# Mixture-of-experts products: tokens as the stationary operand in four column strips, weights as the moving one

## The chip, the cores and the metric

The kernel runs on one core of a Trainium2 chip, in one launch. The metric is the device time in microseconds (us) from the start to the end of an execution; before the change it is 238.63 us, the median of three runs (238.31 to 239.33). In the core, TensorE (PE) multiplies: a load puts a stationary operand into its 128x128 array, then a matmul streams a moving operand past it and writes into PSUM, a memory of eight banks of 512 fp32 columns on 128 partitions. VectorE (DVE) and ScalarE (ACT) read PSUM and write SBUF, the working memory; GpSimd (POOL) works on SBUF alone; DMA queues bring weights from HBM.

## The reference

A small network of two layers over 256 tokens with 192 channels. Each layer is an attention block and then a mixture of eight experts with two experts per token; this change is in the experts alone.

```python
# layer 0: hidden width h = 432, 528, 624, 752, 896, 1088, 1312, 1584
gate = softmax(x @ router.T); val, idx = top_k(gate, 2)
for e in range(8):
    w = sum(where(idx == e, val, 0))
    out += w[:, None] * ((silu(x @ gates[e].T) * (x @ ups[e].T)) @ downs[e].T)
# layer 1: hidden width 768, gates divided by the sum of the two picked
for e in range(8):
    out += tok_w[:, e:e+1] * (relu(x @ w1[e].T + b1[e]) @ w2[e].T + b2[e])
```

All products are fp32.

## The kernel before

Everything is written out by hand: each engine has its own program, in a fixed order, and waits on semaphores. Per layer: norm, attention, norm, router, then the experts. In the experts the router's picks give every token a place among up to 96 (`SLOTS`) places of its expert. PE gathers the tokens of each expert by a product with a matrix of zeros and ones (`gather`, L1183) into PSUM, four experts at a time; ACT and DVE copy the result to `xe_hi` (channels 0 to 127) and `xe_lo` (channels 128 to 191, in two halves of the partitions with zeros between, so that one product can serve gate and up at once). An expert with more than 96 tokens gets the rest in an extra pass; in this run layer 1 has one such job, at the end.

Then come steps, one for each tile of 128 hidden columns of an expert, 60 in layer 0 and 24 in layer 1 (where a step takes two tiles). In `first_products` (L1196, L1198, L1200) the weights, 128 columns of them, are the stationary operand and the 96 tokens the moving one: 96 columns for gate, 192 for the lower channels of both, 96 for up. The hidden values come out with the hidden index on partitions. ACT takes the silu (L521) and DVE the product with up (L786), or each of them adds the bias and takes the relu (L527, L789). That is already the stationary operand of `down` (L1211), with 192 columns of the down weights as the moving one. Two steps (layer 0) or one (layer 1) lie between a step's first products and its `down`, in a ring of four hidden buffers. At the end of an expert DVE copies the 96x192 sum (`y_out`, L775) and `combine` (L1219) multiplies it by the turned gates (`weightedT`: POOL writes `weighted`, L479, PE turns it, L1228, ACT or DVE copies it) into bank 4, where all experts are added up. In layer 1 `L1265` puts the second bias there first.

Every fp32 matmul of the program stands as two in the trace (a transpose as one).

Around it: the weights of all experts of layer 0 are loaded while the attention of layer 0 runs, those of layer 1 after layer 0 is done (`moe_done`), during the attention of layer 1. ACT and DVE read a register and branch before the last expert (to know whether an extra pass follows), PE branches after the last.

Of the kernel before, what the change touches and what calls it, by code (L numbers as in the profile page):

```python
# [42 lines left out]
E = 8  # L43
# [9 lines left out]

HALF = C // 2
# [18 lines left out]
def metaformer_kernel(nc, x_in, weights_hi, weights_lo, weights_mid, params, rel_in, const_in, experts0, experts1,  # L73
                      bias1_in, bias2_in, out):
    with ExitStack() as ctx:
# [66 lines left out]
        weighted = carve(TT * E * SLOTS).rearrange("p (t e s) -> p t e s", t=TT, e=E)  # L142
        weightedT = carve(E * TOK).rearrange("p (e t) -> p e t", e=E)
        xe_hi = carve(E * SLOTS).rearrange("p (e s) -> p e s", e=E)
        hidden = carve(RING * 2 * SLOTS).rearrange("p (r u s) -> p r u s", r=RING, u=2)
        silu_g = carve(2 * SLOTS).rearrange("p (r s) -> p r s", r=2)
        y_out = carve(2 * C).rearrange("p (r c) -> p r c", r=2)

        xe_lo = carve(E * 2 * SLOTS).rearrange("p (e u s) -> p e u s", e=E, u=2)

# [11 lines left out]
        carve_w0(JOB_ROOMS, SIZE1)  # L164
        job_weighted = carve_w0(JOBS, TT, SLOTS)
# [45 lines left out]
        ones_set, zeros_set, half_set = sem("ones_set"), sem("zeros_set"), sem("half_set")  # L211
# [23 lines left out]
        weightedT_psum, weightedT_act, weightedT_vec = sem("weightedT_psum"), sem("weightedT_act"), sem("weightedT_vec")  # L235
# [7 lines left out]
        main = [stream_sems(f"main{layer}") for layer in range(2)]  # L243
# [4 lines left out]

        zeros_job, jobs_ready, job_picked, job_gathered, job_x = (
# [9 lines left out]
        steps1 = [(e, t, P) for e in range(E + JOBS) for t in range(STEPS1)]  # L259
# [3 lines left out]
        main_steps = [range(first_step[layer][E]) for layer in range(2)]  # L263
        TAIL = first_step[0][E - 1]
# [25 lines left out]
        PAIR_AT = (((0, 0), (0, 3), (1, 2), (2, 0)), ((0, 0), (0, 2), (1, 1), (2, 0)))  # L290

        OVER_CHOSEN = 1 + 2 * TT
        OVER_X = 4

        def weightedT_bank(pair):
            return bank[(7, 6, 7, 7)[pair]]
# [4 lines left out]
        PICK_JOB_AT, GATHER_JOB_AT, COPY_JOB_AT = (4, 1), (5, 2), (6, 0)  # L301
# [50 lines left out]
        def tokens_of(e):  # L352

            return (xe_hi[:, e], xe_lo[:, e]) if e < E else (job_xe_hi[:, e - E], job_xe_lo[:, e - E])

        def bias1_of(e, u, t):

            at = u * STEPS1 + t
            return bias1[:, e * TILES1 + at:e * TILES1 + at + 1] if e < E else job_bias[:, e - E, at:at + 1]
# [26 lines left out]
        def _(sp):  # L386
# [8 lines left out]
            for e in range(E):  # L395
                sp.dma_start(w0[:, OFF0[e]:OFF0[e + 1]], experts0[:, OFF0[e]:OFF0[e + 1]]).then_inc(e0_landed[e], 16)
# [6 lines left out]
            for e in range(E):  # L403
                sp.dma_start(w0[:, e * SIZE1:(e + 1) * SIZE1], experts1[:, e]).then_inc(e1_landed[e], 16)

            def load_job(k):

                expert = sp.value_load(job_regs[0:1, 1 + k:2 + k], min_val=0, max_val=E - 1)
                if k >= JOB_ROOMS:

                    sp.wait_ge(main[1]["hidden_used"], first_step[1][E + k - JOB_ROOMS + 1])
# [9 lines left out]
        def _(pool):  # L421
# [6 lines left out]
            for n in range(4):  # L428
# [24 lines left out]
                else:  # L453
                    pool.wait_ge(o_psum, HG * (layer + 1))
                    pool.wait_ge(rstd_ready, n + 1)
                    for half in range(2):
                        if layer + half > 0:
                            pool.wait_ge(zeros_set, 2 * layer + half)
                        nc.gpsimd.memset(xe_lo[CL * half:CL * (half + 1), :, 1 - half, :], 0.0).then_inc(zeros_set, 1)
                    pool.wait_ge(zeros_set, 2 * layer + 2)  # L460
# [16 lines left out]
                    for e in range(E):  # L477
                        for t in range(TT):
                            nc.gpsimd.tensor_scalar(weighted[:, t, e, :], places, place[:, t, e:e + 1], gate[:, t, e:e + 1],  # L479
                                                    ALU.is_equal, ALU.mult).then_inc(weighted_ready, 1)  # L480

        @block.scalar
        def _(act):
# [24 lines left out]
            def copy_weightedT(layer, pair):  # L508
                act.wait_ge(weightedT_psum, 4 * layer + pair + 1)
                nc.scalar.copy(weightedT[0:SLOTS, 2 * pair:2 * pair + 2].rearrange("p e t -> p (e t)"),  # L510
                               weightedT_bank(pair)[0:SLOTS, :]).then_inc(weightedT_act, 1)

            def stream(layer, sems, ns, main_layer=None):

                for n in ns:
# [6 lines left out]
                    elif hidden_by_act(layer, n):  # L522
# [3 lines left out]
                        for u in range(2):  # L526
                            ins = nc.scalar.activation(hidden[:, n % RING, u], up_bank(n)[:, u], ACT.Relu, bias=bias1_of(e, u, t))  # L527
                        ins.then_inc(sems["hidden_act"], 1)
                    if main_layer is not None and (e, t) in PAIR_AT[layer][1::2]:
                        copy_weightedT(layer, PAIR_AT[layer].index((e, t)))  # L530

# [6 lines left out]
            for layer in range(2):  # L538
# [59 lines left out]
                if layer == 1:  # L598
                    act.wait_ge(bias_landed, 32)
                    stream(layer, main[layer], main_steps[layer], layer)  # L600
                    jobs(act, lambda k: stream(1, main[1], steps_of(1, E + k)), lambda k: None)
                else:
                    stream(0, main[0], main_steps[0][:TAIL], 0)
                    most = largest_count(act)
                    with act.If(most > SLOTS):
                        stream(0, main[0], main_steps[0][TAIL:], 0)
                        extra_passes(act, most, lambda i, e: stream(0, over[i], steps_of(0, e)),
                                     lambda i, e: [(over[i]["silu_ready"], len(steps_of(0, e)))])
                    with act.Else():
                        stream(0, main[0], main_steps[0][TAIL:], 0)  # L610
# [3 lines left out]
        def _(dve):  # L614
# [151 lines left out]
            def copy_weightedT(layer, pair):  # L766
# [686 lines left out]
```

## Time and profile before

| | us |
|---|---|
| median of three runs | 238.63 |
| the profiled execution | 239.32 |
| its span, first to last instruction | 237.2 |
| experts of layer 0, first product to the next stage | 60.62 to 136.71 |
| experts of layer 1, first product to the extra job | 180.78 to 224.59 |
| extra job, last sum and the write of the output | 224.59 to 237.2 |

The profile lists each instruction with its start and duration. "x4" at the end of a row means four instructions merged into one row. What follows in brackets is the time the engine sat idle before, and what ended that. A matmul's end in the trace is modelled and overlaps the next one, so the pace of PE is read from start to start. PEld is the load of the stationary operand, which can run beside a matmul.

### The profile page before, as it was taken

How to read it: one execution, taken by the hardware profiler on the slowest of the kernel's cores; microseconds unless marked ns; L12 is line 12 of the kernel's file. 1: busy time of each engine (PE TensorE's matmuls, PEld its weight loads, DVE VectorE, ACT ScalarE, POOL GpSimd, SP SyncE). 2: the span in 40 equal slices, each digit the busy share in tenths (PEclk: the TensorE clock that was granted, in tenths of full speed). 3: DMA queues.
4: the chain of work that ended last, by engine and by line, in shares of the span. 5: the costliest groups of instructions: out<-in, count | busy, mean ns of one | idle time of the engine just before them, and what ended most of it. 6: DMA issues, size and time to landing. Idle time of an engine off the chain costs nothing.

```text
span 237.2 us, 4341 instructions
## 1 busy us (share of the span) xinstructions
PE 217.6 (92%) x1642; PEld 193.2 (81%) x1642; DVE 103.5 (44%) x333; ACT 71.8 (30%) x204; POOL 42.8 (18%) x68
## 2 busy tenths in 40 slices
PE   7799999988999999999989989998979999999961
PEld 7689887576898999999979778765677999999851
DVE  1350687649632222222222243877578284513121
ACT  2241086625222222222212423677231221011000
POOL 1430300027970000000000011200069900000000
PEclk9999999999999999999999999999999999999996
DMA  6999999904000000000000069992000005000001
GB/s 227 390 434 431 438 443 428 418 13 159 3 0 0 3 0 3 0 0 4 0 6 3 0 236 430 424 422 84 3 1 0 3 1 196 6 0 3 0 6 39
DMA packets 4845, 31.16 MB, mean 131 GB/s; under 512 B 648, under 2 KB 2128, under 8 KB 2640
## 3 DMA queue, kind: packets, MB, share of 16 engines
q1 hardware_dynamic: 4240, 30.01, 31.0%
q10 hardware_dynamic: 576, 0.79, 1.1%
q8 instruction: 16, 0.26, 0.5%
q14 instruction: 13, 0.11, 0.1%
HBM read 30.59 MB, written 0.20 MB: 130 GB/s over the span
## 4 chain that ended last, share of the span: by engine, by line
PE 79%; DVE 7%; issue 6%; POOL 2%; ACT 2%; DMA 2%; DVEq 0%; POOLq 0%; ACTq 0%
PE bank L1211 16%; PE bank L1198 12%; PE bank L1196 8%; PE bank L1200 7%; PE bank L961 7%; PE bank L1219 5%; PE bank L1068 4%; PE bank L1029 3%; PE bank L1053 3%; PE bank L1080 3%; PE bank L993 2%; DVE parts L893 2%; DMA x<-x_dram 2%; PE bank L1228 1%; POOL scratch L479 1%
## 5 line engine op out<-in xcount | busy, mean ns | idle before, releaser
L1211 PE MATMUL bank<-w,scratch 128*96 128x192 f32 (+2 forms) x228 | 52.1, 331 | 1.1 <-DVE scratch L786 1.1
L1198 PE MATMUL bank<-scratch,w 128*128 128x192 f32 (+3 forms) x168 | 43.3, 339 | 0.0
L786 DVE TENSOR_TENSOR scratch<-scratch,bank 128x96 f32<-128x96 f32 (+5 forms) x60 | 15.1, 254 | 54.6 <-ACT scratch L521 54.6
L1211 PEld LDWEIGHTS bank<-w,scratch 128*96 128x96 f32 (+2 forms) x228 | 30.6, 164 | 2.9 <-issue 1.4
L521 ACT ACTIVATE scratch<-bank 128x96 f32<-128x96 f32 (+5 forms) x60 | 14.9, 250 | 56.6 <-PE bank L1200 52.5
L1196 PE MATMUL bank<-scratch,w 128*128 128x96 f32 (+3 forms) x168 | 30.8, 265 | 0.1
L1196 PEld LDWEIGHTS bank<-scratch,w 128*128 128x128 f32 (+3 forms) x168 | 27.8, 185 | 3.0 <-issue 3.0
L1200 PE MATMUL bank<-scratch,w 128*128 128x96 f32 (+3 forms) x168 | 29.9, 259 | 0.0
L1200 PEld LDWEIGHTS bank<-scratch,w 128*128 128x128 f32 (+3 forms) x168 | 29.0, 185 | 0.4
L961 PE MATMUL bank<-ones 128*128 128x128 f32 x196 | 27.2, 292 | 1.7 <-POOL ones L424 1.4
L961 PEld LDWEIGHTS bank<-ones 128*128 128x128 f32 x196 | 25.0, 204 | 2.8 <-POOL ones L424 1.4
L1198 PEld LDWEIGHTS bank<-scratch,w 128*128 128x128 f32 (+3 forms) x168 | 24.9, 187 | 0.0
L432 POOL TENSOR_TENSOR rstd<-var_eps,minus_half 128x2 f32<-128x2 f32 x4 | 2.8, 710 | 118.4 <-DVE var_eps L642 118.4
L571 ACT ACTIVATE scratch<-bank,neg_max 128x256 f32<-128x256 f32 x48 | 19.7, 479 | 14.1 <-DVE neg_max L691 13.9
L479 POOL TENSOR_SCALAR scratch<-const,place,gate 128x96 f32<-128x96 f32 x32 | 22.1, 703 | 0.5 <-issue 0.4
L691 DVE TENSOR_REDUCE neg_max<-bank 128x2 f32<-128x512 f32 x24 | 15.7, 683 | 3.1 <-PE bank L1053 3.1
L1068 PE MATMUL bank<-const,scratch 128*128 128x128 f32 x96 | 15.1, 284 | 2.0 <-ACT scratch L571 0.8
L527 ACT ACTIVATE scratch<-bank,bias 128x96 f32<-128x96 f32 x24 | 6.9, 337 | 29.0 <-PE bank L1200 29.0
L1068 PEld LDWEIGHTS bank<-const,scratch 128*128 128x128 f32 x96 | 10.1, 141 | 6.6 <-ACT scratch L571 4.9
L789 DVE TENSOR_SCALAR scratch<-bank,bias 128x96 f32<-128x96 f32 x24 | 6.5, 313 | 20.0 <-PE bank L1200 19.9
L1219 PE MATMUL bank<-scratch 96*128 96x192 f32 x64 | 13.2, 328 | 0.9 <-DVE scratch L775 0.9
L697 DVE COPY scratch<-bank 128x512 f32<-128x512 f32 x16 | 11.0, 684 | 3.2 <-PE bank L1068 3.2
(172 smaller groups left out, 256.4 us busy)
## 6 DMA issues: line engine op xcount, KB each, us to landing
w<-experts_dram SPq DMA_DIRECT2D x9, 1152.0 KB, 11.9
w<-experts_dram SPq DMA_DIRECT2D x1, 3624.0 KB, 40.8
w<-experts_dram SPq DMA_DIRECT2D x1, 3024.0 KB, 32.9
w<-experts_dram SPq DMA_DIRECT2D x1, 2496.0 KB, 26.2
w<-experts_dram SPq DMA_DIRECT2D x1, 2016.0 KB, 20.8
w<-experts_dram SPq DMA_DIRECT2D x1, 1704.0 KB, 16.8
w<-experts_dram SPq DMA_DIRECT2D x1, 1416.0 KB, 12.3
w<-experts_dram SPq DMA_DIRECT2D x1, 1272.0 KB, 9.4
```

Source lines behind the costliest of these rows:

```text
L479: nc.gpsimd.tensor_scalar(weighted[:, t, e, :], places, place[:, t, e:e + 1], gate[:, t, e:e + 1], ALU.is_equal, ALU.mult).then_inc(weight ...
L521: nc.scalar.activation(silu_g[0:m, n % 2, :], up_bank(n)[0:m, 0], ACT.Silu).then_inc(sems["silu_ready"], 1)
L571: nc.scalar.activation(probs[:, h % HB, t, :], bank[h % HB][:, t * TOK:(t + 1) * TOK], ACT.Exp, bias=neg_max[:, h, t:t + 1]).then_inc(prob ...
L691: nc.vector.tensor_reduce(neg_max[:, h, :], bank[h % HB][:].rearrange("p (t k) -> p t k", t=TT), AX_X, ALU.max, negate=True).then_inc(max_ ...
L786: nc.vector.tensor_tensor(hidden[0:m, n % RING, 0], silu_g[0:m, n % 2, :], up_bank(n)[0:m, 1], ALU.mult).then_inc(sems["hidden_vec"], 1)
L961: nc.tensor.matmul(bank[b][:, 0:P], ones[:], ones[:], start=True, stop=True)
L1068: last = nc.tensor.transpose(bank[4 + head % 2][:, at:at + P], probs[:, h % HB, t, k * P:(k + 1) * P], ident)
L1196: nc.tensor.matmul(tile[:, 0], w0[:, begin + long[0]:begin + long[0] + m], hi, start=True, stop=False, skip_group_check=True)
L1198: nc.tensor.matmul(tile.rearrange("p u s -> p (u s)"), w0[:, begin + short:begin + short + m], lo.rearrange("p u s -> p (u s)"), start=Fal ...
L1200: return nc.tensor.matmul(tile[:, 1], w0[:, begin + long[1]:begin + long[1] + m], hi, start=False, stop=True, skip_group_check=True)
L1211: ins = nc.tensor.matmul(y_bank(e)[0:SLOTS, 0:C], hidden[0:m, n % RING, u], w0[0:m, begin + at:begin + at + C], start=t == 0 and u == 0, s ...
L1219: ins = nc.tensor.matmul(bank[4][:, t * C:(t + 1) * C], turned[0:SLOTS, t * P:(t + 1) * P], y_out[0:SLOTS, e % 2, :], start=first and t == ...
```

## The change

The roles are swapped. 32 places of tokens (`UNIT`) are the stationary operand in one of four column strips of the array (`tile_position=(0, 32 * q)`), and the weights stream past, up to 512 columns of them at once. Strips 0 to 2 hold the three units of a "wide" expert, strip 3 works through the three units of a "narrow" one, so that 24 units make six groups of four (`WIDE`, `NARROW`). Both streams of hidden tiles have 45 blocks of 128 columns in layer 0 and 36 in layer 1; they are cut into macros of 4 blocks (12 macros, the last with one block) and of 6 blocks (6 macros). A macro has four parts on PE: `first_upper` (channels 0 to 127, gate and up), the turn of the macro before, `first_lower` (channels 128 to 191 for gate in the upper half of the rows and for up in the lower half, written to two banks) and `down_main` of the macro before. The hidden values now come out with tokens on partitions, so `turn_hidden` turns them on PE, four or six 128x128 transposes a macro, and ACT (in layer 1 ACT and DVE) copies them to `hT`, before `down_main` can use them as its stationary operand. Bias of layer 1 comes from a table `bias1_of` that is spread over the slots; it adds a DMA of 128x4608 fp32. The zeros in `xe_lo` go, and with them POOL's memsets (L459). `weighted` is laid out by group, so there are three rounds of turns in place of four and six combines in place of eight. The extra job keeps the old form.

```diff
+UNIT = 32
+WIDE = ((1, 2, 3, 4, 5, 7), (2, 3, 4, 5, 6, 7))
+NARROW = ((0, 0, 0, 6, 6, 6), (0, 0, 0, 1, 1, 1))
+MACRO = (4, TILES1)
+HALF1 = HID1 // 2
...
+            def first_upper(layer, m):
...
+                for which in range(2):
+                    for q in range(QUADS):
+                        rows = slice(UNIT * q, UNIT * (q + 1))
+                        for i, b, n, col in pieces_of(layer, q, m):
+                            e = expert_of(layer, q, i)
...
+                            nc.tensor.matmul(first_bank(m, which)[rows, to:to + wide], xe_hi[:, e, tokens_at(q, i)], w0[:, at:at + wide],
+                                             start=col == 0, stop=False, tile_position=(0, UNIT * q), skip_group_check=True)
+            def first_lower(layer, m):
+                for q in range(QUADS):
+                    rows = slice(UNIT * q, UNIT * (q + 1))
+                    for i, b, n, col in pieces_of(layer, q, m):
...
+                        for which in range(2):
+                            part = slice(CL * which, CL * (which + 1))
+                            last = nc.tensor.matmul(first_bank(m, which)[rows, to:to + wide], xe_lo[part, e, tokens_at(q, i)],
+                                                    w0[part, at:at + wide], start=False, stop=True, tile_position=(CL * which, UNIT * q),
+                                                    skip_group_check=True)
+                last.then_inc(main[layer]["first_psum"], 1)
+            def turn_hidden(layer, m):
...
+                    pe.wait_ge(sems["h_ready"], m + 1)
+                    if m > 0:
+                        pe.wait_ge(sems["hT_act"], m)
+                    for b in range(len(blocks_of(0, 0, m))):
+                        last = nc.tensor.transpose(bank[7][:, b * P:(b + 1) * P], gated[:, b * P:(b + 1) * P], ident)
+                    last.then_inc(sems["hT_psum"], 1)
...
+            def down_main(layer, m):
+                sems = main[layer]
+                pe.wait_ge(sems["hT_act"], m + 1)
+                count = len(blocks_of(layer, 0, m))
+                for col in range(count):
+                    if layer == 1 and col == STEPS1:
+                        pe.wait_ge(sems["hT_vec"], m + 1)
+                    for q in range(QUADS):
...
+                        last = nc.tensor.matmul(y_bank_of(layer, i)[UNIT * q:UNIT * (q + 1), 0:C], hT[0:k, col, UNIT * q:UNIT * (q + 1)],
+                                                w0[0:k, at:at + C], start=b == 0, stop=b + 1 == tiles_of[layer][e],
+                                                tile_position=(0, UNIT * q), skip_group_check=True)
...
+                for m in range(MACROS[layer]):
+                    first_upper(layer, m)
+                    if m > 0:
+                        turn_hidden(layer, m - 1)
...
+                    if 1 <= m <= 3:
+                        turn_weighted(layer, m - 1)
...
+                    for i in range(GROUPS):
+                        if combined_at(layer, i) == m:
+                            combine_main(layer, i)
+                    first_lower(layer, m)
+                    if m > 0:
+                        down_main(layer, m - 1)
...
 # ScalarE, a macro: copy_turned(m - 1), then (layer 0) silu(m)
+                    nc.scalar.copy(hT[:, 0:n].rearrange("p b s -> p (b s)"), bank[7][:, 0:n * P]).then_inc(sems["hT_act"], 1)
+                nc.scalar.activation(gated[:, 0:n], first_bank(m, 0)[:, 0:n], ACT.Silu).then_inc(sems["silu_ready"], 1)
...
 +                    if layer == 1 and m > 0:
+                        copy_turned(m - 1)
+                    if 1 <= m <= 3:
+                        copy_weightedT(layer, m - 1)
+                    if layer == 0:
...
+                        nc.vector.tensor_tensor(gated[:, 0:n], gated[:, 0:n], first_bank(m, 1)[:, 0:n], ALU.mult).then_inc(sems["h_ready"], 1)
+                    else:
...
+                            nc.vector.tensor_tensor(gated[:, cols], first_bank(m, half)[:, 0:HALF1], bias1_of[:, m, cols], ALU.add).then_inc(sems["h_ready"], 1)
+                    if m > 0:
+                        copy_sums(layer, m - 1)
...
+        BEFORE_TAIL = (MACROS[0] - 2, MACROS[1] - 1)
```

On PE, in the middle of layer 0, the program before has one step after another, of which three stand here (`bank<-scratch,w` is a first product, `bank<-w,scratch` a `down`).

```order
L1196 MATMUL bank<-scratch,w 128x96
L1198 MATMUL bank<-scratch,w 128x192
L1200 MATMUL bank<-scratch,w 128x96
L1211 MATMUL bank<-w,scratch 96x192
L1196 MATMUL bank<-scratch,w 128x96
L1198 MATMUL bank<-scratch,w 128x192
L1200 MATMUL bank<-scratch,w 128x96
L1211 MATMUL bank<-w,scratch 96x192
```

At the same place the changed program has macros; these are macros 6 and 7 (L1396 is `first_upper`, L1424 `turn_hidden`, L1411 `first_lower`, L1452 `down_main`, L1371 `combine_main`).

```order
L1396 MATMUL bank<-w,scratch 32x512 x8
L1424 MATMUL bank<-const,scratch 128x128 x4
L1411 MATMUL bank<-w,scratch 32x512 x8
L1452 MATMUL bank<-w,scratch 32x192 x16
L1396 MATMUL bank<-w,scratch 32x512 x8
L1424 MATMUL bank<-const,scratch 128x128 x4
L1371 MATMUL bank<-scratch 128x192 x2
L1411 MATMUL bank<-w,scratch 32x512 x8
L1452 MATMUL bank<-w,scratch 32x192 x16
```

Full-array instructions (the turn, the combine) now stand between instructions that use strips, and the two strip forms follow each other. The second place on PE is macro 2 of layer 0, where the wide strips change from one expert to the next and the narrow strip does not.

```order
L1396 MATMUL bank<-w,scratch 32x256 x6
L1396 MATMUL bank<-w,scratch 32x512
L1396 MATMUL bank<-w,scratch 32x256 x6
L1396 MATMUL bank<-w,scratch 32x512
L1424 MATMUL bank<-const,scratch 128x128 x4
L1362 MATMUL bank<-const,scratch 128x128 x4
L1411 MATMUL bank<-w,scratch 32x256 x12
L1411 MATMUL bank<-w,scratch 32x512 x2
L1452 MATMUL bank<-w,scratch 32x192 x16
```

Here two matmuls of the same strip follow each other before the next strip's come. The third place is ACT around its branch in layer 0, near the end (L597 is the silu, L588 the copy of the turned values).

```order
L588 COPY scratch<-bank 128x512
L597 ACTIVATE scratch<-bank 128x512
L384 TENSOR_LOAD counts
L384 ISA x2
L697 COMPARE_AND_BRANCH
L588 COPY scratch<-bank 128x512
L597 ACTIVATE scratch<-bank 128x512
L588 COPY scratch<-bank 128x512
L597 ACTIVATE scratch<-bank 128x128
L588 COPY scratch<-bank 128x128
```

The branch now stands two macros before the end, between a silu and the copy that `down_main` of the same macro waits for.

## Rows read from the trace of the kernel before

**Rows 1.** The page, busy time, share of the span and instructions of the engines.

```profile
PE 217.6 (92%) x1642; PEld 193.2 (81%) x1642; DVE 103.5 (44%) x333; ACT 71.8 (30%) x204; POOL 42.8 (18%) x68
```

**Rows 2.** Stages: us; busy PE, PEld, DVE, ACT, POOL; granted clock; DMA share; GB/s.

```profile
60.60:136.60 76.00, 74.47 (x528) 69.64 (x528) 19.65 (x72) 17.56 (x64) 8.90 (x14) 1.00 0.01 2
...
180.80:224.60 43.80, 43.25 (x304) 41.92 (x303) 18.91 (x72) 8.04 (x26) 9.27 (x14) 1.00 0.08 28
```

**Rows 3.** Timeline of PE, one step of layer 0: start us, us, line, shapes.

```profile
125.50 0.36 PE L1196 MATMUL bank<-scratch,w 128*128 128x96 f32 x2
...
126.25 0.49 PE L1211 MATMUL bank<-w,scratch 128*96 128x192 f32 x2
126.57 0.36 PE L1196 MATMUL bank<-scratch,w 128*128 128x96 f32 x2
```

**Rows 4.** Timeline of PE, the end of a step of layer 1.

```profile
218.99 0.36 PE L1196 MATMUL bank<-scratch,w 128*128 128x96 f32 x2
...
219.73 0.82 PE L1211 MATMUL bank<-w,scratch 128*96 128x192 f32 x4
220.38 0.36 PE L1196 MATMUL bank<-scratch,w 128*128 128x96 f32 x2
```

**Rows 5.** Chain that ended last: start us, us on the chain, engine, line.

```profile
27.42 1.97 PE bank L1053 x30
...
36.32 1.00 PE bank L1080 x16
...
77.67 0.65 PE bank L1219 x4
...
182.51 0.84 PE bank L1265 x4
...
211.85 0.83 PE bank L1183 x8
```

**Rows 6.** Timeline of PE, two row halves of the array (L1007).

```profile
13.52 1.57 PE L1007 MATMUL bank<-xnT,att_lo 64*128 64x256 f32 x12
```

**Rows 7.** Timeline of PE, first step of layer 0 and a turn of gates.

```profile
60.62 0.43 PE L1196 MATMUL bank<-scratch,w 128*128 128x96 f32 x2
...
61.43 0.60 PE L1228 MATMUL bank<-const,scratch 128*96 128x128 f32 x4
61.87 0.25 PE L1196 MATMUL bank<-scratch,w 128*128 128x96 f32 x1
```

**Rows 8.** Timelines of ACT and DVE, layer 0: copies out of PSUM.

```profile
65.63 0.58 ACT L510 COPY scratch<-bank 96x512 f32<-96x512 f32 x1 [0.69 <-PE bank L1228]
62.09 0.68 DVE L768 COPY scratch<-bank 96x512 f32<-96x512 f32 x1
135.29 0.35 DVE L775 COPY scratch<-bank 96x192 f32<-96x192 f32 x1 [0.79 <-PE bank L1211]
```

**Rows 9.** Timelines of ACT, DVE and PE after the branch of layer 0.

```profile
120.85 0.39 ACT L521 ACTIVATE scratch<-bank 128x96 f32<-128x96 f32 x2 [3.05 <-issue]
121.93 0.42 DVE L786 TENSOR_TENSOR scratch<-scratch,bank 128x96 f32<-128x96 f32 x2 [3.86 <-ACT scratch L521]
122.33 0.54 PE L1211 MATMUL bank<-w,scratch 128*96 128x192 f32 x2 [1.07 <-DVE scratch L786]
```

**Rows 10.** The page, GB/s in 40 equal slices of the span (5.93 us each).

```profile
GB/s 227 390 434 431 438 443 428 418 13 159 3 0 0 3 0 3 0 0 4 0 6 3 0 236 430 424 422 84 3 1 0 3 1 196 6 0 3 0 6 39
```

**Rows 11.** Timeline of PE, the ends of both layers.

```profile
135.70 0.92 PE L1219 MATMUL bank<-scratch 96*128 96x192 f32 x4 [0.45 <-DVE scratch L775]
136.71 0.48 PE L961 MATMUL bank<-ones 128*128 128x128 f32 x2
224.59 0.43 PE L1196 MATMUL bank<-w 128*128 128x96 f32 x2
```

**Rows 12.** Timeline of PE's loads, one `weigh` of attention (L1080).

```profile
36.25 0.59 PEld L1080 LDWEIGHTS bank<-scratch,v 128*32 128x32 f32 x16 [0.17 <-issue]
```

**Rows 13.** The same loads as one group: count, ns min/median/max, first and last start.

```profile
L1080 PEld LDWEIGHTS bank<-scratch,v x16: 106/110/110, 36.2 to 36.7; 128*32 128x32 f32 x16
```

More of the change, by code:

```diff
@@ new lines, in pieces_of, with finished_in @@
+        def pieces_of(layer, q, m):
+            pieces = []
+            for col, (i, b) in enumerate(blocks_of(layer, q, m)):
+                if pieces and pieces[-1][0] == i:
+                    pieces[-1][2] += 1
+                else:
+                    pieces.append([i, b, 1, col])
+            return pieces
+        def finished_in(layer, part, m):
+            return [i for i, b in blocks_of(layer, 0 if part == 0 else UNITS, m)
+                    if b + 1 == tiles_of[layer][(WIDE, NARROW)[part][layer][i]]]
@@ new lines, in combined_at, with columns_of, first_bank, y_bank_of @@
+        def combined_at(layer, i):
+            m = max(m for part in range(2) for m in range(MACROS[layer]) if i in finished_in(layer, part, m))
+            return max(4, m + 2)
+        def columns_of(layer, m):
+            return P * len(blocks_of(layer, 0, m))
+        def first_bank(m, which):
+            return bank[2 * (m % 2) + which]
+        def y_bank_of(layer, i):
+            return bank[5 + (i % 2 if layer == 0 else 0)]
+        WEIGHTED_ORDER = [(0, 0), (1, 0), (0, 1), (0, 2), (1, 3), (0, 3), (0, 4), (0, 5)]
@@ L775, in copy_y, with stream @@
                 nc.vector.tensor_copy(y_out[0:SLOTS, e % 2, :], y_bank(e)[0:SLOTS, 0:C]).then_inc(sems["y_ready"], 1)
-            def stream(layer, sems, ns, end):
+            def stream(layer, sems, ns):
                 for n in ns:
@@ new lines, in turn_hidden @@
+            def turn_hidden(layer, m):
+                sems = main[layer]
+                if layer == 0:
+                    pe.wait_ge(sems["h_ready"], m + 1)
[4 more added lines that the diff above has]
+                    last.then_inc(sems["hT_psum"], 1)
+                else:
+                    for half in range(2):
+                        pe.wait_ge(sems["h_ready"], 2 * m + half + 1)
+                        if m > 0:
+                            pe.wait_ge(sems["hT_vec" if half else "hT_act"], m)
+                        for b in range(STEPS1):
+                            at = half * HALF1 + b * P
+                            last = nc.tensor.transpose(bank[6 + half][:, b * P:(b + 1) * P], gated[:, at:at + P], ident)
+                        last.then_inc(sems["hT_psum"], 1)
@@ L1279, in one @@
[L1279 to L1291 removed]
+                            pe.wait_ge(bias_landed, 48)
@@ L1293, in extra @@
+                    if layer == 1 and m == MACROS[1] - 1:
+                        gather_job(0)
+                m = MACROS[layer]
+                turn_hidden(layer, m - 1)
+                for i in range(GROUPS):
+                    if combined_at(layer, i) == m:
+                        combine_main(layer, i)
+                down_main(layer, m - 1)
+                if layer == 0:
+                    combine_main(0, GROUPS - 1)
             def extra(i, e):
```

386 lines of the change are left out of this document (230 added, 156 removed).

## The prediction

> **What bounds the kernel now.** I read the page's busy times first: PE works in 92% of the span, no other engine that computes in more than 44% [rows 1]. Then the stages: in the experts of layer 0 PE is busy 74.5 of 76.0 us, in those of layer 1 43.25 of 43.8, at a granted clock of 1.00, the level of 2.4 GHz [rows 2]. So the experts take what PE's matmuls take, and a change there is priced by what PE streams. Next the timeline of PE. A step of layer 0 comes every 1.07 us (125.50 to 126.57) and streams 96 + 192 + 96 columns and 192 for `down`, 576 in all, each in two passes [rows 3]. In layer 1 a step takes 1.39 us (218.99 to 220.38) for 768 columns; the four passes of its two `down` matmuls take 0.65 us, so a column costs 0.65 / (4 x 192) = 0.85 ns a pass [rows 4]. By that price the steps would be 0.98 and 1.31 us; the rest is small overhead. Nothing waits: PE is the bound by the number of columns. Half of the 192 columns of the lower channels are zeros, and the 96 tokens fill three quarters of the array in `down`; that is what swapping the roles can save.
>
> Then I looked for strips of the array in the trace. `weigh` (L1080) puts 32 columns in each of four strips: 16 passes of 256 columns take 1.00 us of the chain [rows 5]. One after another they would take 16 x 256 x 0.85 = 3.48 us, in fours 0.87. So four strips do stream at the same time, and 0.13 us is left for going over to the strips. Two row halves (L1007) also share the array: 12 passes of 256 columns last 1.57 us, where 2.61 would be due in a row and 1.31 in pairs [rows 6]; a tenth of a us more is the start, the rest the drain of the last.
>
> **Streams.** Four strips work through 45 blocks in layer 0. A block is 256 columns of upper channels, 128 of lower ones (gate and up in the two row halves at once) and 192 of `down`, again 576. That is 45 x 576 x 2 x 0.85 = 44.1 us. In layer 1 a macro is 2 x 384 + 384 + 6 x 192 = 2304 columns; six take 6 x 2304 x 2 x 0.85 = 23.5 us. Both rest on eight tiles, two row halves by four strips, streaming together in `first_lower`. The rows show four strips alone and two halves alone, never both. If the halves take turns, 45 x 128 + 6 x 384 = 8064 columns come twice: 13.7 us more. I take 0, since each kind of tile by itself comes within 0.15 us of full overlap, and keep 13.7.
>
> **Added and removed beside them.** Turning the hidden values: 45 and 36 transposes. Four transposes take 0.44 us from start to start (61.43 to 61.87) [rows 7], 0.11 each, so 5.0 and 4.0 us, all on PE's path. Turns of the gates: three rounds of four, 1.3 us a layer (before four rounds). Combines: 0.65 us each [rows 5], six, 3.9 us a layer (before eight). The second bias (0.84) and the gather of the job (0.83, and two turns of 0.22) stay [rows 5].
>
> **Going between forms.** Every macro goes from strips to the full array for the turn, to row halves by strips for `first_lower`, and back to strips for `down_main`: three changes, 39 in layer 0 with first and last macro, 21 in layer 1; before there is none in the experts. The two rows above give 0.13 and 0.10 us for going in; for going out none is as clear. I take 0.15 a change, 5.9 and 3.1 us; the ends are 0.10 and 0.26 (out as dear as in), that is 3 us less or 6.6 more.
>
> **Uneven pieces.** In macros 1, 2, 5 and 8 of layer 0 a strip gets two matmuls in a row before the next strip's come. If the later strip can start past the waiting one, it costs nothing; if it can't, the three wide strips of macros 1, 2 and 5 go one after another, 1.74 us more in each of three rounds (3 x 0.87 in place of 0.87), 3 x 5.2 = 16 us. In `weigh` eight matmuls of two passes in 1.00 us show that a strip's second pass, due 0.22 us later, doesn't hold back the next strip, so I take 1.5 us, near the low end. The Trainium skill, "TensorE: Matmul & The Clock Gate", section "Part 3: Packing small matmuls", says that matmuls start and end strictly in program order. By that rule the 16 us would be due, and, where the two passes of a matmul stand side by side, `weigh` would take 9 x 0.22 = 2.0 us; the trace has 1.00.
>
> **Waits.** PE turns macro m only after `down_main` of m-1 (1.3 us) and `first_upper` of m+1 (1.74). In that time ACT takes a silu of 512 columns (0.58 by its copy of that size) and DVE the product (0.68) [rows 8]; with hand-overs of about 0.3 that is 1.6 of 3.0 us, hidden. The turn's copy (0.58 and 0.25 of hand-over) lies beside `first_lower` and two changes of form, 0.87 + 0.3: hidden with 0.3 us to spare; without that cover a macro would pay up to 0.8. `down_main` has `first_upper` and the combines queued behind it, so a late copy delays all. The last macro has no cover: copy of one block (0.5 with hand-over), two y copies (0.35 each) and their hand-over, the last drain: 1.7 us. For the end of layer 1, where the job's first products follow, 0.3.
>
> The branch of ACT and DVE in layer 0 now costs PE 1.07 us, with ACT away 3.05 [rows 9]. In the new order ACT takes it after a silu, 3.2 us before the next copy falls due; I cost it at nothing, at most at 1. In layer 1 DVE branches before the last macro, after copies and `pick_job`, and comes back some 0.7 us after `down_main` needs its half of the copy (0 to 1.5). The bias table is 2.36 MB; the queue moves about 430 GB/s [rows 10], so 5.5 us, loaded in the attention of layer 1, where the four slices of weights leave some 20 us free. POOL's memsets aren't waited for.
>
> **Sum.** Layer 0: 44.1 + 5.0 + 1.3 + 3.9 + 5.9 + 1.5 + 1.7 = 63.4 us, against 76.1 from 60.62 to 136.71 [rows 7, 11]: 12.7 less. Layer 1: 23.5 + 4.0 + 1.3 + 3.9 + 0.8 + 1.1 + 3.1 + 0.3 + 0.7 = 38.7, against 43.8 from 180.78 to 224.59 [rows 2, 11]: 5.1 less. Nothing else moves. The profiled execution took 239.32 us (span 237.2), so 239.3 - 17.8 = 221.5; the median shown is 0.7 lower, 238.63, and the forecast for a median is 221 us.
>
> **Rivals.** *The row halves take turns* in `first_lower`: 221 + 13.7 = 235. For it: no row with eight tiles. Against it: both forms overlap singly. Chance 0.10.
>
> *Strips held back in order* at uneven pieces: 221 + 14.5 = 235. For it: in those macros a strip's second matmul waits for a whole first one, not for a pass of it. Against it: `weigh`. Chance 0.06.
>
> *The pace of instructions*. `down_main` needs a new pass every 0.04 us. The densest long stretch shown, the scores (L1053), has 30 in 1.97 us, 0.066 each [rows 5]. If that is a limit, 32 passes take 2.1 and not 1.3 us in 11 macros, 48 take 3.15 and not 1.95 in six: 16 us, 237. Against it: 16 loads of `weigh` lie within 0.59 us [rows 12]. Chance 0.06.
>
> *Loads that don't hide*, the slower side. All four strips use all rows of the array. If a strip's load had to wait until the array's rows are free, each group of four passes would pay a load of 0.11 us [rows 13]. There are 14 groups in a macro of layer 0 and 18 in layer 1, 11.25 x 14 + 6 x 18 = 265: 29 us, 250. It turns the change slower from 17.8 / 265 = 0.067 us a group on. Against it: four groups in 1.00 us leave 0.13 in all; but those have 256 columns to hide a load behind, `down_main` 192 and the pieces 128. The Trainium skill says, on the same page and section, that a load overlaps matmuls in flight only where their row groups differ; the row of `weigh` differs from that rule. Chance 0.07.
>
> **Chances and range.** The forecast, with its own range of 214 to 227 (changes of form at 0.10 and no waits, to changes at 0.26), has 0.71. The rivals at 235 to 237 have 0.22 (0.16 of it at 235), the slower one 0.07. A measurement here can't tell under 0.5%, 1.2 us, from no change. Faster by more is the forecast, two of the rivals and half of the third, 0.90; no change 0.03; slower 0.07. The range for 8 in 10 is 213 to 236: it holds the forecast's own and the two rivals at 235, and leaves out the two above.
>
> **What would show it.** Right: 16 `down_main` matmuls of a macro from first to last start in 1.3 us, `first_upper` in 1.74, `first_lower` in 0.87, four starts within some hundredths of a us; about 0.1 us extra at each change of form; a macro of layer 0 in 4.8 us, 5.4 with a combine; the experts in about 63 and 39 us. Wrong: `first_lower` as long as `first_upper`; macros 1, 2 and 5 several us longer than 3; loads starting only after the passes before them end; PE waiting for ACT's copy in every macro.

## The result, and the profile after

The changed kernel takes 224.28 us, the median of four runs (222.52 to 224.38), against 238.93 for the kernel before on the same chip (four runs, 238.31 to 239.33): 0.937 of its time, with an interval of 0.932 to 0.942. The forecast was 221 us with a range of 213 to 236. The profiled execution took 224.36 us, 15.0 less than the 239.32 of before; the forecast for that difference was 17.8.

PE still bounds the kernel. This is the page's row of busy times, for [rows 1]: PE's 217.6 us have become 203.7, in 649 more instructions.

```profile
PE 203.7 (92%) x2291; PEld 139.0 (63%) x2291; DVE 102.6 (46%) x285; ACT 64.0 (29%) x146; POOL 39.8 (18%) x64
```

Next come the stages of the changed kernel, for [rows 2]: experts of layer 0, attention of layer 1, experts of layer 1 (us; busy PE, PEld, DVE, ACT, POOL; granted clock; DMA share; GB/s).

```profile
60.60:126.20 65.60, 63.86 (x914) 31.97 (x906) 14.52 (x28) 14.94 (x26) 8.64 (x13) 1.00 0.01 3
126.20:171.50 45.30, 40.93 (x324) 32.53 (x324) 28.85 (x86) 20.75 (x53) 7.68 (x11) 0.97 0.64 262
171.50:208.50 37.00, 37.00 (x564) 22.62 (x562) 23.28 (x68) 2.94 (x6) 9.24 (x14) 1.00 0.10 34
```

From first product to next stage, as in the prediction, the trace gives this:

| stage | before | forecast | after | after - before |
|---|---|---|---|---|
| up to the experts of layer 0 | 60.62 | 60.62 | 60.23 | -0.4 |
| experts of layer 0 | 76.1 | 63.4 | 66.0 | -10.1 |
| attention of layer 1 | 44.1 | 44.1 | 45.4 | +1.3 |
| experts of layer 1 | 43.8 | 38.7 | 37.0 | -6.8 |
| job, last sum, output | 12.6 | 12.6 | 13.7 | +1.1 |

So three things need a reason: layer 0 is 2.6 us longer than the sum, the attention of layer 1 lost 1.3 us although no line of it was changed, and the granted clock of that stage is 0.97. The job and the end are taken up at the close. The mechanism itself is there. The timeline of PE shows two macros of layer 0 in a row; they answer to the steps of [rows 3].

```profile
95.75 2.08 PE L1452 MATMUL bank<-w,scratch 128*32 128x192 f32 x32
97.64 1.90 PE L1396 MATMUL bank<-w,scratch 128*32 128x512 f32 x16
99.47 0.66 PE L1424 MATMUL bank<-const,scratch 128*128 128x128 f32 x4
99.96 0.82 PE L1371 MATMUL bank<-scratch 128*128 128x192 f32 x4
100.71 1.09 PE L1411 MATMUL bank<-w,scratch 64*32 64x512 f32 x16
101.73 0.37 PE L1452 MATMUL bank<-w,scratch 128*32 128x192 f32 x4
```

Read from start to start, `first_upper` (L1396) takes 1.83 us, the turn (L1424) 0.49, `first_lower` (L1411) 1.02: eight tiles do stream together. But `down_main` (L1452) takes 1.89 us here, and only 1.32 in the next macro, which has a combine. The same in a table by macro, of `down_main` alone (us, busy PE and PEld, granted clock):

```profile
67.08:68.94 1.86, 1.86 (x32) 1.05 (x32) 1.00 0.04 9
72.92:74.93 2.01, 2.00 (x32) 0.96 (x32) 1.00 0.00 0
...
85.46:86.79 1.33, 1.33 (x32) 0.94 (x32) 1.00 0.00 0
...
95.75:97.64 1.89, 1.89 (x32) 0.95 (x32) 1.00 0.00 0
```

The long ones have no combine ahead of them; I first took this for a late copy of ACT and a slow supply of instructions behind it. The timeline of PE's loads inside one of them says otherwise:

```profile
67.91 0.29 PEld L1452 LDWEIGHTS bank<-w,scratch 128*32 128x32 f32 x6
68.50 0.13 PEld L1452 LDWEIGHTS bank<-w,scratch 48*32 48x32 f32 x2 [0.30 <-issue]
68.94 0.18 PEld L1396 LDWEIGHTS bank<-w,scratch 128*32 128x32 f32 x8 [0.30 <-DVE scratch L889]
```

The break stands around one strip of 48 rows: expert 0 is 432 wide, so its last block has 432 - 384 = 48 hidden values. Its loads come 0.30 us after the others, and the next ones 0.30 us after them. The last block of layer 0 has strips of 48 rows beside one of 32, and the loads break there too:

```profile
123.14 0.15 PEld L1452 LDWEIGHTS bank<-w,scratch 48*32 48x32 f32 x6 [0.55 <-ACT scratch L588]
123.59 0.13 PEld L1452 LDWEIGHTS bank<-w,scratch 32*32 32x32 f32 x2 [0.30 <-issue]
```

### The profile page after: what moved, and what is told of

Its sections match the earlier page's. It is cut to its first block, busy times and chain, and to the rows that moved or that the text cites. A ratio compares the mean times of both kernels' runs of the same rounds, so it can differ in the third digit from the quotient of the medians.

```text
span 222.2 us, 5411 instructions
## 1 busy us (share of the span) xinstructions
PE 203.7 (92%) x2291; PEld 139.0 (63%) x2291; DVE 102.6 (46%) x285; ACT 64.0 (29%) x146; POOL 39.8 (18%) x64
## 4 chain that ended last, share of the span: by engine, by line
PE 79%; DVE 7%; issue 6%; ACT 2%; DMA 2%; POOL 2%; DVEq 0%; POOLq 0%; ACTq 0%
PE bank L1452 15%; PE bank L1396 13%; PE bank L1411 7%; PE bank L1092 7%; PE bank L1199 4%; PE bank L1371 4%; PE bank L1160 4%; PE bank L1184 3%; PE bank L1424 3%; PE bank L1314 3%; PE bank L1211 3%; PE bank L1124 3%; PE bank L1433 2%; DMA x<-x_dram 2%; PE bank L1362 1%
## 5 line engine op out<-in xcount | busy, mean ns | idle before, releaser
L1452 PE MATMUL bank<-w,scratch 128*32 128x192 f32 (+4 forms) x648 | 33.7, 329 | 0.7 <-ACT scratch L588 0.7
L1452 PEld LDWEIGHTS bank<-w,scratch 128*32 128x32 f32 (+4 forms) x648 | 19.5, 109 | 18.6 <-issue 10.5
L1396 PE MATMUL bank<-w,scratch 128*32 128x512 f32 (+3 forms) x332 | 31.0, 493 | 0.0
L889 DVE TENSOR_TENSOR scratch<-scratch,bank 128x512 f32<-128x512 f32 (+1 forms) x12 | 7.9, 655 | 37.3 <-ACT scratch L597 37.3
L1396 PEld LDWEIGHTS bank<-w,scratch 128*32 128x32 f32 x332 | 11.1, 109 | 11.9 <-issue 9.3
L1411 PE MATMUL bank<-w,scratch 64*32 64x512 f32 (+3 forms) x332 | 17.8, 497 | 0.0
L588 ACT COPY scratch<-bank 128x512 f32<-128x512 f32 (+1 forms) x12 | 6.7, 559 | 36.5 <-PE bank L1424 36.5
L877 DVE COPY scratch<-bank 32x192 f32<-32x192 f32 (+1 forms) x24 | 8.6, 358 | 12.1 <-PE bank L1452 11.8
L1199 PEld LDWEIGHTS bank<-const,scratch 128*128 128x128 f32 x96 | 10.1, 141 | 6.6 <-ACT scratch L664 4.9
L597 ACT ACTIVATE scratch<-bank 128x512 f32<-128x512 f32 (+1 forms) x12 | 6.9, 571 | 13.1 <-PE bank L1411 13.1
L1371 PE MATMUL bank<-scratch 128*128 128x192 f32 x48 | 9.7, 334 | 1.0 <-DVE scratch L877 0.9
L1314 PE MATMUL bank<-parts 128*128 128x384 f32 (+1 forms) x40 | 8.4, 343 | 1.9 <-POOL parts L532 1.8
L1184 PE MATMUL bank<-parts 32*128 32x256 f32 x96 | 8.9, 302 | 0.4 <-POOL parts L528 0.4
## 6 DMA issues: line engine op xcount, KB each, us to landing
w<-experts_dram SPq DMA_DIRECT2D x1, 1416.0 KB, 12.6
```

Of the source, the lines that this page charges most:

```text
L1184: last = nc.tensor.matmul(bank[b][:, t * TOK:(t + 1) * TOK], left[rows, g, t * P:(t + 1) * P], right[rows, g, :] if right is not None else ...
L1199: last = nc.tensor.transpose(bank[4 + head % 2][:, at:at + P], probs[:, h % HB, t, k * P:(k + 1) * P], ident)
L1314: last = nc.tensor.matmul(out_ap, part[:, t, c * P:(c + 1) * P], tokens(t), start=i == 0 and t == 0, stop=i == 1 and t == TT - 1)
L1371: ins = nc.tensor.matmul(bank[4][:, t * C:(t + 1) * C], weightedT[:, i, t * P:(t + 1) * P], y_out[:, i % 3, :], start=layer == 0 and i == ...
L1396: nc.tensor.matmul(first_bank(m, which)[rows, to:to + wide], xe_hi[:, e, tokens_at(q, i)], w0[:, at:at + wide], start=col == 0, stop=False ...
L1411: last = nc.tensor.matmul(first_bank(m, which)[rows, to:to + wide], xe_lo[part, e, tokens_at(q, i)], w0[part, at:at + wide], start=False, ...
```

## Experiments

**128 rows in every block.** The down weights past an expert's width are zeros already, so the sums stay.

```diff
-                        k = min(P, HID0[e] - b * P) if layer == 0 else P
+                        k = P
```

> `down_main` of the changed kernel takes all 128 rows in every block of layer 0; the weights of the rows past an expert's width are zeros, so the sums stay. In the trace after, five macros of layer 0 lose 0.55 to 0.68 us and one 0.25 just where a strip has 48, 16, 32 or 64 rows, and the last macro 0.45. Theory (a strip with few rows is another form of the array, it can't stream beside strips of 128 rows, so it waits for them, runs alone and is waited for): 0.55 + 0.68 + 0.55 + 0.57 + 0.25 + 0.57 + 0.45 = 3.6 us less, 224.3 - 3.6 = 220.7 us, `down_main` 1.32 us in all eleven macros of 16 matmuls. Rival (the pace at which PE gets its instructions after a late wait, as those macros have no combine ahead of them): 224.3, the gaps stay.

Measured: 219.07 us (five runs, 218.78 to 220.29), ratio to the kernel before 0.917 (0.9145 to 0.9194). `down_main` of the same macro has lost its gap, as the timeline of PE in that run shows (67.01 to 68.33):

```profile
67.01 1.51 PE L1452 MATMUL bank<-w,scratch 128*32 128x192 f32 x32
68.33 1.08 PE L1396 MATMUL bank<-w,scratch 128*32 128x256 f32 x12
```

It is 1.32 us in ten of the eleven macros with 16 matmuls, with or without a combine (the eleventh, at the end, 1.44). All `down_main` of layer 0 together, each read to the start of the next row, fall from 19.90 to 16.17 us, 3.7 less. That is the theory's 3.6; the slow supply of instructions is out. The layer as a whole is 3.9 shorter (65.96 to 62.05 us): the macro with strips of 64 rows, put down above with 0.25, loses 0.57, part of it after its `down_main` row ends. The median fell by 5.2, and the rest goes with the granted clock: four of these runs had a mean granted clock of 0.992 to 0.993 (218.8 to 219.3 us) and one 0.984 (220.29), where the changed kernel had 0.983 to 0.984 in three (224.2 to 224.4) and 0.990 in one (222.52). At like clocks the gain is 3.9 to 4.1 or 3.3 to 3.7 us.

**65 rows.**

```diff
+                        k = min(P, max(HID0[e] - b * P, 65)) if layer == 0 else P
```

> As the run with 128 rows everywhere, but a short block takes at least 65 rows (48, 16, 64 and 32 become 65; 112 stays). If every height over 64 is the full form (112 rows cost nothing in the trace after), the time is that of 128 rows, 220.7 us. If the form goes by steps of 32 rows, or by any height below 128, the gaps stay, 224.3 us.

Measured: 219.72 us (two runs, 218.74 and 220.70), 0.920 (0.914 to 0.925), and again 1.32 to 1.33 us in the ten macros. 65 rows do what 128 do, and 64 (macro 7 of the changed kernel) do not; so beside strips of 128 the step lies between 64 and 65.

**Tiles of like and of unlike height.**

```diff
+                        k = CL if layer == 0 else P if q < UNITS else CL
```

> `down_main` of the changed kernel leaves out half of the hidden values: in layer 0 all four strips take 64 rows in every block, in layer 1 strips 0 to 2 take 128 and strip 3 takes 64. Theory (tiles of unlike height can't stream together, tiles of like height can): layer 0 loses its gaps, 3.6 us less, and the change of form moves from ahead of `down_main` to behind it; in layer 1 each of 36 groups of four takes 0.70 us in place of 0.163, 19.4 us more; 240 us. Rival (the gaps belong to the last block of an expert, not to its rows): 224.3 us, layer 0 keeps its gaps and layer 1 its 37.0 us.

Measured: 241.59 us. In layer 1, where one strip of four is lower, the loads stop at each of its matmuls and `down_main` takes 5.37 us (174.42 to 179.79) for 1.97; first the loads, then PE:

```profile
174.88 0.14 PEld L1452 LDWEIGHTS bank<-w,scratch 64*32 64x32 f32 x2 [0.30 <-issue]
175.32 0.15 PEld L1452 LDWEIGHTS bank<-w,scratch 128*32 128x32 f32 x6 [0.30 <-issue]
```

```profile
76.56 1.09 PE L1411 MATMUL bank<-w,scratch 64*32 64x512 f32 x16
77.45 1.50 PE L1452 MATMUL bank<-w,scratch 64*32 64x192 f32 x32
78.88 1.49 PE L1396 MATMUL bank<-w,scratch 128*32 128x512 f32 x12
...
174.42 5.44 PE L1452 MATMUL bank<-w,scratch 128*32 128x192 f32 x48
179.79 1.18 PE L1396 MATMUL bank<-w,scratch 128*32 128x384 f32 x12
```

That is (5.37 - 1.97) / 6 = 0.57 us for each group of four matmuls, and 20.1 in all six macros (32.2 for 12.1), where I expected 19.4 (my "0.70 for 0.163" left out that a group has two passes; the price was right, the base was not). In layer 0, where all four strips have 64 rows, nothing stops within `down_main`, and the change of form has moved as expected: `first_lower`, which has 64 rows too, hands over after 0.89 us for 1.02, and the way from `down_main` to `first_upper` costs 0.1 more (1.43 for 1.32). So it is unlike height that can't stream together, not a low tile, and a change of form goes with a change of the tile's size.

**The clock at the end of layer 0.** The timeline of PE at that end in the changed kernel, for the first row of [rows 11], and then the granted clock (the seventh number behind the stretch, ahead of DMA share and GB/s):

```profile
123.14 0.96 PE L1452 MATMUL bank<-w,scratch 48*32 48x192 f32 x8 [0.35 <-ACT scratch L588]
125.03 1.00 PE L1371 MATMUL bank<-scratch 128*128 128x192 f32 x4 [0.93 <-DVE scratch L877]
126.19 4.98 PE L1092 MATMUL bank<-ones 128*128 128x128 f32 x30 [0.16 <-issue]
```

```profile
125.00:126.00 1.00, 0.97 (x4) 0.62 (x4) 0.00 (x0) 0.00 (x0) 0.00 (x0) 0.84 0.08 16
126.00:128.00 2.00, 1.84 (x9) 1.82 (x9) 1.54 (x7) 0.00 (x0) 0.07 (x1) 0.50 0.23 37
128.00:129.00 1.00, 1.00 (x7) 1.00 (x6) 0.31 (x2) 0.12 (x1) 0.65 (x1) 0.50 0.76 157
129.00:130.00 1.00, 1.00 (x10) 1.00 (x10) 0.37 (x2) 0.76 (x2) 0.00 (x0) 0.95 0.93 387
```

After waits of 0.30, 0.35 and 0.93 us the clock goes to its lower level, 1.2 GHz, and stays there for some three us, across the 30 passes that open layer 1. The experiment puts `keep_clock` matmuls into these waits:

```diff
                     first_lower(layer, m)
+                    if layer == 0 and m == MACROS[0] - 1:
+                        keep_clock(1, 0)
...
+                if layer == 0:
+                    keep_clock(1, 0)
                 down_main(layer, m - 1)
                 if layer == 0:
+                    keep_clock(4, 0)
                     combine_main(0, GROUPS - 1)
```

> Six matmuls of 128 columns on ones are put into PE's waits at the end of layer 0: one ahead of each of the last two `down_main`, four ahead of the last combine; nothing else changes. In the trace after PE is idle there for 0.30, 0.36 and 0.93 us, the granted clock falls to 0.50 from 125.8 to 129.05 us, and the 30 passes at the start of layer 1 take 4.71 us where they took 3.33. Theory (the idle end of layer 0 costs the clock of the next stage): granted clock 1.00 through 130 us, the 30 passes in 3.3 us, 224.3 - 1.5 = 222.8 us. Rival (the clock falls for another reason, such as the DMAs that start there): the clock still falls, 224.3 us or up to 0.5 more for fillers longer than their waits.

Measured: 222.82 us (four runs, 222.59 to 223.07), 0.933 (0.9305 to 0.9356). The waits are filled, the combine starts at 125.03 as before, and the 30 passes run from 126.05 to 129.49, 3.4 us where it was 4.8 (126.19 to 131.01), at a granted clock of 1.00:

```profile
124.03 1.16 PE L1092 MATMUL bank<-ones 128*128 128x128 f32 x8
125.03 0.89 PE L1371 MATMUL bank<-scratch 128*128 128x192 f32 x4
126.05 3.61 PE L1092 MATMUL bank<-ones 128*128 128x128 f32 x30
129.49 0.27 PE L1105 MATMUL bank<-const,xn 128*128 128x128 f32 x1
```

```profile
126.00:130.00 4.00, 3.95 (x34) 3.80 (x34) 2.21 (x10) 0.88 (x2) 0.72 (x1) 1.00 0.56 175
```

The DMAs start there as before, so they weren't the cause, and this accounts for the 1.3 us of the attention. In the strip-by-strip run below, the clock is at 0.50 behind the same waits while no DMA is at work (the 0.00 behind it is the DMA share):

```profile
167.00:169.00 2.00, 2.00 (x9) 2.00 (x9) 0.54 (x3) 0.00 (x0) 0.00 (x0) 0.50 0.00 0
```

The waits alone don't decide it, though. In the profiled run with 65 rows PE waits 0.30, 0.36, 0.96 and 0.30 us at the same end, and the granted clock stays at 1.00 through the 30 passes, which take 3.45 us (122.24 to 125.69). First PE's timeline there, then the granted clock:

```profile
122.24 3.61 PE L1092 MATMUL bank<-ones 128*128 128x128 f32 x30 [0.30 <-issue]
```

```profile
122.00:126.00 4.00, 3.76 (x33) 3.77 (x34) 2.21 (x10) 0.88 (x2) 0.72 (x1) 1.00 0.57 170
```

Of the seven profiled runs with these waits, six show the fall; neither of the two with fillers does. By its time, one of the four runs of the changed kernel (222.52 us) seems to have kept the clock as well, so the gain of 1.5 us in the median is that of a fall that comes often and not always. What decides it without fillers is not shown.

**Both products in one row half.** This prices the assumption on which 13.7 us of the forecast stood.

```diff
-                    nc.tensor.matmul(first_bank(m, which)[rows, to:to + wide], xe_lo[part, e, tokens_at(q, i)],
-                                     w0[part, at:at + wide], start=False, stop=True, tile_position=(CL * which, UNIT * q),
+                    nc.tensor.matmul(first_bank(m, which)[rows, to:to + wide], xe_lo[0:CL, e, tokens_at(q, i)],
+                                     w0[0:CL, at:at + wide], start=False, stop=True, tile_position=(0, UNIT * q),
```

> `first_lower` of the changed kernel takes gate and up both from the upper half of the rows (the up product of the lower channels is computed with gate's weights, so that part of the computation is changed); number and size of the matmuls stay. Theory (in the changed kernel the two halves stream side by side): `first_lower` of 16 passes 0.87 to 1.74 us, 13.7 us more in all, 238 us. Rival of the forecast (the halves took turns already): 224.3, no change.

Measured: 244.69 us, 20.3 more than the changed kernel's profiled run. Where macros are even the price is exact: `first_lower` takes 1.87 us (84.20 to 86.07) for 1.02. In layer 1 all of it rises from 4.84 to 8.67 us, 3.8 for the 3.9 due. The rest is in the three uneven macros, which pay 10.4 us in place of 2.6, as the first row of PE's timeline shows for one (3.23 us to the next row, for 1.06 in the changed kernel):

```profile
66.79 3.30 PE L1411 MATMUL bank<-w,scratch 64*32 64x128 f32 x28
70.02 0.37 PE L1452 MATMUL bank<-w,scratch 128*32 128x192 f32 x4
...
84.20 1.94 PE L1411 MATMUL bank<-w,scratch 64*32 64x512 f32 x16
86.07 1.95 PE L1452 MATMUL bank<-w,scratch 128*32 128x192 f32 x32
```

There a strip has eight passes in a row ahead of the next strip. Its first five start at 66.791, 66.925, 67.034, 67.142 and 67.252; the next strip's first starts at 67.258. So strips do hold each other, from some number of passes on.

**Order of the pieces.** Two kernels cut every macro of layer 0 into four pieces of 128 columns a strip; the second deals them out in turn.

```diff
-                if pieces and pieces[-1][0] == i:
+                if layer == 1 and pieces:
```

```diff
-                    for q in range(QUADS):
+                    for k in range(len(pieces_of(layer, 0, m))):
+                      for q in range(QUADS):
...
-                        for i, b, n, col in pieces_of(layer, q, m):
+                        i, b, n, col = pieces_of(layer, q, m)[k]
```

> The changed kernel with every macro of layer 0 cut into four pieces of 128 columns a strip, in the order strip by strip: 8 passes of a strip stand before the first of the next one. In the run with one half of the rows, 8 passes of one strip in a row let the next strip start only with the fifth (67.252 and 67.258 us); in the changed kernel, with 4, the starts of four strips lie within 50 ns. Theory (a strip takes four passes ahead, the fifth holds up all behind it): `first_upper` 8 x 0.44 + 0.44 = 3.9 us for 1.74, `first_lower` 4 x 0.44 + 0.44 = 2.2 for 0.87, 3.5 x 11.25 = 39 us more, 263 us. By strict order of starts: a strip's 7 x 0.11 us before the next one starts, 6.3 and 3.2 us, 77 more, 302 us. If strips never hold each other: 224.3 us.

> The same pieces of 128 columns in the order piece by piece, a strip's next pass after those of all other strips. Both theories of holding: 224 to 226 us, `first_upper` 1.85 us with its change of form. Rival of the forecast (PE gets a new pass only every 0.066 us): 64 passes take 4.2 us in place of 1.74 and of 0.87, 66 us more, 290 us.

Measured: 262.3 us strip by strip, 221.85 in turn (one run each; a mean granted clock of 0.99 in both). A macro of the first and one of the second kernel:

```profile
67.41 4.19 PE L1396 MATMUL bank<-w,scratch 128*32 128x128 f32 x63
71.53 0.66 PE L1424 MATMUL bank<-const,scratch 128*128 128x128 f32 x4
...
72.55 2.48 PE L1411 MATMUL bank<-w,scratch 64*32 64x128 f32 x64
74.97 1.94 PE L1452 MATMUL bank<-w,scratch 128*32 128x192 f32 x32
```

```profile
63.23 1.95 PE L1397 MATMUL bank<-w,scratch 128*32 128x128 f32 x64
65.11 0.65 PE L1426 MATMUL bank<-const,scratch 128*128 128x128 f32 x4
...
66.14 1.16 PE L1413 MATMUL bank<-w,scratch 64*32 64x128 f32 x64
67.22 1.94 PE L1454 MATMUL bank<-w,scratch 128*32 128x192 f32 x32
```

Strip by strip `first_lower` takes 2.42 us and `first_upper` 4.26 (67.27 to 71.53; the row's first pass fell before the window), close to the 2.2 and 3.9 of the theory. Strips begin 0.467 us apart: the first begins at 86.535, its fifth pass at 86.995, the next strip at 87.001. In turn the same pieces take 1.88 and 1.08. Sixty-four passes in 1.08 us is one every 0.017, so the pace of instructions is no limit here. Between the two orders layer 0 differs by 40.8 us (107.4 and 66.6), where the theory has 39.

The 221.85 us are no gain of the pieces: layer 0 takes 66.6 us in that run and 66.0 in the changed kernel. What differs is the end of the program, where PE's wait ahead of the last combine is 3.01 us in the changed kernel and 0.45 in this run (0.44 strip by strip, 2.59 to 2.81 in the other runs). By that, 2.6 us, both measured times are shorter, and why the wait is short in these two kernels is not shown. The changed kernel, then the run in turn:

```profile
217.12 0.99 PE L1350 MATMUL bank<-scratch,w 96*128 96x192 f32 x4 [3.01 <-issue]
```

```profile
215.20 0.92 PE L1350 MATMUL bank<-scratch,w 96*128 96x192 f32 x4 [0.45 <-DVE scratch L917]
```

**The parts together.**

```diff
+            return MACROS[0] if layer == 0 and i == GROUPS - 2 else max(4, m + 2)
...
+                    if layer == 0:
+                        i, sems = GROUPS - 1, main[0]
+                        act.wait_ge(sems["down_done"], MACROS[0])
+                        act.wait_ge(sems["combined"], i - 2)
+                        nc.scalar.copy(y_out[SLOTS:P, i % 3, :], y_bank_of(0, i)[SLOTS:P, 0:C]).then_inc(sems["narrow_ready"], 1)
...
+                        k = P
...
+                        keep_clock(1, 0)
...
+                    keep_clock(2, 0)
```

> The changed kernel with 128 rows in every `down_main` (219.07 us by itself), the clock held at the end of layer 0 (one filler ahead of the next to last `down_main`, two ahead of the last combine), the fifth combine moved from macro 10 into the wait for the last `down_main` (0.36 us of idle time), and the last copy of the narrow strip given to ACT beside DVE's copy of the wide ones (0.36 us). Theory (each of these is time on PE's path): 219.07 - 0.36 - 0.36 = 218.3 us, a granted clock of 0.99 in all runs. Rival (ACT's copy waits for its table load, or the combine is late): 219 us or more.

Measured: 218.00 us (five runs, 217.49 to 218.16), 0.9133 (0.9117 to 0.9149): faster than both kernels. The end of layer 0 has no idle PE left up to the last combine (L1378; fillers are L1099); the experts of layer 0 take 61.2 us (60.26 to 121.41), the attention behind them 44.0.

```profile
119.73 0.71 PE L1099 MATMUL bank<-ones 128*128 128x128 f32 x4
120.32 0.89 PE L1378 MATMUL bank<-scratch 128*128 128x192 f32 x4
121.41 2.83 PE L1099 MATMUL bank<-ones 128*128 128x128 f32 x23 [0.21 <-issue]
```

## Why the prediction was right, point by point

*Streams: right.* The price of 0.85 ns a column and pass held: `first_upper` 1.74 us and its change of form, `down_main` 1.32 once the heights are alike, 1.97 to 2.09 in layer 1 for 1.95. That eight tiles stream together was the boldest step, and it is shown: with one row half instead of two an even macro pays the 0.87 us.

*Blocks with few rows: no term at all, and the step that failed.* I wrote that 45 blocks of 192 columns cost the same each. Five experts end in a block of 64 rows or fewer, and where they do, a strip of unlike height stops the other three. It is 3.9 us of layer 0 (65.96 with them, 62.05 with 128 rows in every block), more than the whole miss there. The shapes stood in the reference (432, 528, 1088, 1312 and 1584) and `k` in the diff.

*Changes of form: right in kind, near in size.* The trace has a gap of 0.08 to 0.10 us at each of the three changes of a macro and none from `down_main` to `first_upper`. A macro without a combine takes 4.77 us at 128 rows (99.26 to 104.03 in that run, forecast 4.8), which leaves (4.77 - 4.35) / 3 = 0.14 a change, with the slower first pass of each new form. 39 such changes are 5.5 us for the 5.9 forecast.

*Uneven pieces: small as forecast, for a reason I had only half.* In macros 1, 2 and 5 `first_upper` takes 1.90 us for the 1.83 of even ones and `first_lower` 1.06 for 1.02; in macro 8, where only the narrow strip changes, nothing. That is 0.3 us in all, where I put 1.5. I said that a later strip can start past the waiting one. It can, as long as no strip has more than four passes in a row in one row half, and the changed kernel never has more. With eight, strips are held back: 40.8 us between the two orders. The Trainium skill, "TensorE: Matmul & The Clock Gate", section "Part 3: Packing small matmuls", says that matmuls start and end strictly in program order; here the next strip's first pass starts (87.001) before the sixth to eighth of the strip ahead of it (87.105 and later), so here the starts are not in program order.

*Waits: right.* The copy of ACT ends 0.33 us before `down_main` starts in macros without a combine, as forecast. The end of layer 0 had waits of 0.30, 0.35 and 0.93 us and 0.16 behind the last combine, 1.7 forecast and measured. The branch of layer 1 cost nothing where I put 0.7.

*"Nothing else moves": wrong, 2.4 us.* The thin end of layer 0 cost the next stage its clock, 1.3 us (a wait was priced by its length alone). And the sixth combine of layer 1 wasn't removed but moved behind the first products of the job: 0.72 us there (209.56 to 210.28), with 0.26 more of waiting at the end (3.01 for 2.75, which is within what the runs differ by there). That makes layer 1 look 0.7 us better than it is.

*Sum.* Forecast against measured: short blocks +3.9, uneven pieces -1.2, changes -0.4, layer 1 with its moved combine -1.7, job and end +1.1, clock +1.3, the start -0.4. That is +2.6 where 15.0 for 17.8 is +2.8; the rest stays below what I can split. So 6.3 us that the forecast lacked met 3.7 that it had too much, and that the total came so close is in part luck. The forecast's own range had a slip at its low end: changes at 0.10 and no waits give 221 - 3.0 - 2.7 = 215, not 214.

*Rivals.* Row halves that take turns, loads that don't hide (32 loads of `down_main` in 1.13 us) and the pace of instructions are each ruled out by a run. Strips held back is true from the fifth pass on, which this kernel doesn't reach.

## What to carry to other kernels

When small tiles are packed into the array, list the height of each stationary tile: in these runs tiles of 64 rows or fewer don't overlap with tiles of 128, nor one of 32 with tiles of 48, and one such tile among four costs about 0.55 us; padding it with zeros cost nothing. Deal work to strips in turn, never more than four passes of one tile in a row. And when a stage is made shorter, look at PE's waits at its end: an idle end can be paid for again in the next stage through the clock (1.3 us here), and fillers in waits that exist anyway cost nothing measurable here.

## What the runs showed that was not expected

The step between 64 and 65 rows: 16, 32, 48 and 64 rows stop strips of 128, 65 and 112 don't (0.55 us each against none). A strip of 32 rows stops strips of 48 too, so there is a further step between 32 and 48: the last block's matmuls last 0.96 us and, with like heights, 0.53. A strip takes four passes ahead: with eight in a row strips start 0.467 us apart, 0.134 for the first pass and three of 0.109, plus 0.006. And behind waits of 0.30, 0.35 and 0.93 us PE fell to half its clock for some three us; with fillers in the same waits it did not, and in one run without fillers (65 rows) it did not either.
